# Delta-rule layers: one tile per engine loop, single buffers with copies by ScalarE, and a 64-column set that makes a product and the fourth power

## The chip, the cores and the metric

The kernel runs on one core of one Trainium2 chip. The metric is device time in microseconds (us) of one execution, as the median of several. The engines are PE (TensorE), DVE (VectorE), ACT (ScalarE), POOL (GpSimd) and SP (SyncE); each works through its own list of instructions, and semaphores order them against each other.

## The reference, cut to what matters

The whole model is a chain of a convolution block, a halo attention, a delta-rule transformer, a top-k memory, an attention with mixed heads and a mixture of experts, on 4 x 1024 tokens of 256 channels. The change touches the delta-rule layers alone. There are two of them, with 8 heads of 32:

```python
def delta_rule(q, k, v, beta):
    def step(W, inp):
        qt, kt, vt, bt = inp
        wk = jnp.einsum('bhde,bhe->bhd', W, kt)
        v_new = bt * (vt - wk)
        W = W + jnp.einsum('bhd,bhe->bhde', v_new, kt)
        out = jnp.einsum('bhde,bhe->bhd', W, qt)
        return (W, out)
    W0 = jnp.zeros((bsz, H, D, D), dtype=q.dtype)
    _, outs = jax.lax.scan(step, W0, (q, k, v, beta))
    return outs
...
q = jax.nn.softmax(q, axis=-1); k = jax.nn.softmax(k, axis=-1); beta = jax.nn.sigmoid(beta)
```

## The kernel before, in words

`fast_weight_stage` (L581) runs once per layer. A tile is 32 time steps of all 4 sequences, 128 rows; there are NT = 32 tiles. Within a tile the 32 steps of the scan are solved at once: a lower triangular 32 x 32 system for each of 4 sequences and 8 heads. So nearly all products are *sets* of 32 products of 32 x 32 (8 heads by 4 sequences), which the helper `tiles` (L659) writes out.

Three things run side by side, one tile apart each: the projections and softmax of tile i+1 (`project`, `less_max`, `softmax`), the factors of the triangular system of tile i (`gram`, L673, and five sets called `product`: l8 by l8t, z1 by l2, z2 by l2, tt by l2, z3 by loff), and for tile r = i-1 the recurrence (`chain` sets that read the state M, solve, and step M at L847; then the output `att`). `body(i, ...)` writes one such step for an engine. `bodies` (L613) writes five bodies out, then an engine loop (`Fori`) whose turn holds **four** bodies, then five bodies again; buffers that live longer than a body have four (`qk`, `qkT`, `vh`) or two (`z3`, `nt`, `qm`) places and are indexed by the tile's number mod 4 or 2. The order on each engine is that of the code; PE waits at the head of a set, never inside one.

Other stages have loops too. The mixed-head attention (names with `hm_`) has a PE loop over the four sequences whose body holds an inner loop of six turns (`block_of_queries`): in the built program one inner turn is 748 PE instructions, and the whole body around it 2,486 (each written instruction counted once).

Of the kernel before, what the change touches and what calls it, by code (L numbers as in the profile page):

```python
# [17 lines left out]
P = 128  # L18
# [562 lines left out]
def fast_weight_stage(k, layer, H):  # L581
# [6 lines left out]
    with ExitStack() as ctx:  # L588
# [9 lines left out]
        l8, l8t, loff, z1, z2, tt, l2 = (compact(n) for n in "l8 l8t loff z1 z2 tt l2".split())  # L598
        z3, nt, qm = (sb(n, [P, 2, HEADS, STEP]) for n in ("z3", "nt", "qm"))
        u0, r0, rk, U, M, att = (compact(n) for n in "u0 r0 rk U M att".split())  # L600
        names = ("w power staged pq pv dif exp root qk ga l8 lo qm t l2 z2 tt z3 nt th u0 so r0 rk u m up in att ot fin "
                 "go dch pch").split()
        (s_w, s_power, s_staged, s_pq, s_pv, s_dif, s_exp, s_root, s_qk, s_ga, s_l8, s_lo, s_qm, s_t, s_l2, s_z2, s_tt,
         s_z3, s_nt, s_th, s_u0, s_so, s_r0, s_rk, s_u, s_m, s_up, s_in, s_att, s_ot, s_fin, s_go, s_dch, s_pch) = (
# [8 lines left out]
        def bodies(body, eng, start=None):  # L613

            for i in range(-1, 4):
                body(i, i % 4, i + 1 < NT, i >= 0, i >= 1)
            with eng.Fori(1, NT // 4 - 1) as j:
                if start:
                    start()
                for a in range(4):  # L620
                    body(j * 4 + a, a, True, True, True)
            if start:
                start()
            for i in range(NT - 4, NT + 1):
                body(i, i % 4, i + 1 < NT, i < NT, True)
# [4 lines left out]
        with nc.Block() as block:  # L630
# [5 lines left out]
            def _(pool):  # L636
                own = Steps(pool, s_pch)

                def body(i, a, nxt, ch, rc):
# [15 lines left out]
            def _(pe):  # L655
# [14 lines left out]
                def gram(a):  # L670
                    for n in range(HEADS):
                        for b in range(B):
                            mm = pe.matmul(bank[2][rows(b), 2 * STEP * n:2 * STEP * n + 2 * STEP],  # L673
                                           qkT[rows(b), a, HEADS + n, :], qkT[rows(b), a, n:2 * HEADS:HEADS, :],
                                           start=True, stop=True)
                    mm.then_inc(s_ga, 1)

                of = lambda ap: (lambda n: ap[:, n, :])
                product = lambda left, right: tiles(lambda n: bank[3][:, cols(n)], of(right), of(left), s_t)
                chain = lambda by, moving, sig: tiles(lambda n: bank[4][:, cols(n)], by, of(moving), sig)  # L680

                def body(i, a, nxt, ch, rc):
                    r, ra, ru = i - 1, (a - 1) % 4, (a - 1) % 2
                    if rc:
                        pe.wait_ge(s_m, r + 1)
                        pe.sem_inc(s_go, 1)
                        chain(lambda n: qkT[:, ra, HEADS + n, :], M, s_th)
                    if ch:
# [4 lines left out]
                        gram(a)  # L693
                    if rc:
# [3 lines left out]
                        chain(lambda n: z3[:, ru, n, :], u0, s_so)  # L698
# [3 lines left out]
                    if rc:  # L702
                        pe.wait_ge(s_r0, r + 1)
                        pe.sem_inc(s_go, 1)
                        chain(lambda n: nt[:, ru, n, :], r0, s_so)
# [4 lines left out]
                    if rc:  # L710
                        pe.wait_ge(s_rk, r * 2 + 1)
                        pe.sem_inc(s_go, 1)
                        chain(lambda n: nt[:, ru, n, :], rk, s_so)
                    if nxt:
                        project(i + 1, QKN, 3 * C + HEADS, 1, s_pv)
                    if ch:
                        pe.wait_ge(s_l2, i + 1)
                        pe.sem_inc(s_go, 1)
                        product(z1, l2)
                    if rc:  # L720
                        pe.wait_ge(s_rk, r * 2 + 2)
                        pe.sem_inc(s_go, 1)
                        chain(lambda n: nt[:, ru, n, :], rk, s_so)
                    if ch:
                        pe.wait_ge(s_z2, i + 1)
                        pe.sem_inc(s_go, 1)
                        product(z2, l2)
                    if rc:
                        if since(r, 1):
                            pe.wait_ge(s_att, r)  # L730
                        pe.sem_inc(s_go, 1)
                        tiles(lambda n: bank[6][:, cols(n)], lambda n: qkT[:, ra, n, :], of(M), None, stop=False)
                        pe.wait_ge(s_u, r + 1)
                        pe.sem_inc(s_go, 1)
                        tiles(lambda n: bank[5][:, cols(n)], lambda n: qk[:, ra, C + STEP * n:C + STEP * n + STEP],
                              of(U), s_up)
                    if ch:
                        pe.wait_ge(s_tt, i + 1)
                        pe.sem_inc(s_go, 1)
                        product(tt, l2)  # L740
                    if rc:
                        for n in range(HEADS):
                            for b in range(B):
                                mm = pe.matmul(bank[6][rows(b), cols(n)], qm[rows(b), ru, n, :], U[rows(b), n, :],
                                               start=False, stop=(n == HEADS - 1))
                        mm.then_inc(s_in, 1)
                    if ch:
# [3 lines left out]
                        product(z3[:, a % 2], loff)  # L751
# [13 lines left out]
            def _(act):  # L765
                def body(i, a, nxt, ch, rc):
# [4 lines left out]
                    if ch:  # L771
                        act.wait_ge(s_t, i * 5 + 1)
                        act.activation(flat(l2[:, :, :]), bank[3][:, 0:C], ACT.Copy).then_inc(s_l2, 1)
                    if nxt:
# [10 lines left out]
                    if ch:  # L785
                        act.wait_ge(s_t, i * 5 + 5)
                        act.activation(flat(nt[:, a % 2, :, :]), bank[3][:, 0:C], ACT.Copy, scale=-1.0).then_inc(s_nt, 1)
# [10 lines left out]
            def _(dve):  # L798
# [13 lines left out]
                def softmax(i, a):  # L812
                    dve.wait_ge(s_exp, i + 1)
                    own.done(dve.tensor_reduce(sm[:, :], groups(ex[:, :]), AX.X, ALU.add))
                    own.done(dve.reciprocal(rs[:, :], sm[:, :]))
                    dve.wait_ge(s_root, i + 1)
                    own.mark(dve.tensor_tensor(split(vh[:, a, :]), split(bank[1][:, 0:C]), wide(eb[:, 2, :], HEADS),
                                               ALU.mult))
                    own.done(dve.tensor_tensor(rs[:, HEADS:16], rs[:, HEADS:16], eb[:, 2, :], ALU.mult))
                    own.done(dve.tensor_tensor(groups(qk[:, a, :]), groups(ex[:, :]), wide(rs[:, :], 16), ALU.mult))  # L820
                    dve.transpose(qkT[:, a, :, :].rearrange("p n j -> p (n j)"), qk[:, a, :]).then_inc(s_qk, 1)

                def lower(i):
# [3 lines left out]
                    dve.tensor_tensor(z1[:, :, :], small(2), l8t[:, :, :], ALU.subtract).then_inc(s_l8, 1)  # L827

                def masks(u):
                    dve.tensor_tensor(loff[:, :, :], pairs[:, :, 1, :], off, ALU.mult).then_inc(s_lo, 1)  # L830
                    dve.tensor_tensor(qm[:, u, :, :], pairs[:, :, 0, :], small(3), ALU.mult).then_inc(s_qm, 1)

                def factor(i, n, to, before, sig):
                    dve.wait_ge(s_t, i * 5 + n)
                    dve.tensor_tensor(to, split(bank[3][:, 0:C]), before[:, :, :], ALU.add).then_inc(sig, 1)

                def corrected(r, ra):
                    dve.wait_ge(s_th, r + 1)
                    dve.tensor_tensor(flat(u0[:, :, :]), vh[:, ra, :], bank[4][:, 0:C], ALU.subtract).then_inc(s_u0, 1)  # L839
# [9 lines left out]
                def body(i, a, nxt, ch, rc):  # L849
                    r, ra = i - 1, (a - 1) % 4  # L850
                    if rc:
                        corrected(r, ra)
# [4 lines left out]
                    if ch:  # L857
                        masks(a % 2)
# [4 lines left out]
                    if ch:  # L863
                        factor(i, 2, z2[:, :, :], z1, s_z2)
                    if rc:
                        solution(r, 4, U, s_u)
# [1499 lines left out]
```

## Time and profile before

| what | us |
|---|---|
| median of 3 runs | 5422.78 (5417.58 to 5423.65) |
| profiled execution, its own time | 5467.1 |
| its span, first to last instruction | 5465.3 |
| first delta layer, 328 to 1258 of the span | 930 |
| second delta layer, 1636 to 2552 of the span | 916 |

The profiled execution is 0.8% longer than the median of the runs. In the profile PE is the busiest engine (77% of the span); in the two delta layers all engines have idle time. A line such as `L659 PE MATMUL psum<-fw_M,fw_qkT 32*32 32x32 f32` is a group of matmuls with the tiles that they read; "idle ... <-issue" is time in which the engine waited for nothing that the profile shows.

### The profile page before, as it was taken

How to read it: one execution, taken by the hardware profiler on the slowest of the kernel's cores; microseconds unless marked ns; L12 is line 12 of the kernel's file. 1: busy time of each engine (PE TensorE's matmuls, PEld its weight loads, DVE VectorE, ACT ScalarE, POOL GpSimd, SP SyncE). 2: the span in 40 equal slices, each digit the busy share in tenths (PEclk: the TensorE clock that was granted, in tenths of full speed). 3: DMA queues.
4: the chain of work that ended last, by engine and by line, in shares of the span. 5: the costliest groups of instructions: out<-in, count | busy, mean ns of one | idle time of the engine just before them, and what ended most of it. 6: DMA issues, size and time to landing. Idle time of an engine off the chain costs nothing. (4 is left out here: it accounts for less than half of the span.)

```text
span 5465.3 us, 173116 instructions
## 1 busy us (share of the span) xinstructions
PE 4194.9 (77%) x75148; PEld 2525.7 (46%) x75149; DVE 2689.1 (49%) x5011; ACT 1812.7 (33%) x3259; POOL 877.7 (16%) x2195
## 2 busy tenths in 40 slices
PE   3666666667986666666788887699999999984995
PEld 1235455453435555554245554255454544533663
DVE  3443223233023323332478887378685886852343
ACT  1121111112121111110366665167575775731221
POOL 0000000000000000000155554011111111104012
PEclk7776666667996666666899998799999999995997
DMA  1000000000000000000100000000000000005123
GB/s 41 2 8 4 4 4 4 4 4 18 0 6 4 4 4 4 4 4 5 37 1 1 1 1 1 9 1 0 1 0 1 0 1 1 0 3 210 61 83 101
DMA packets 47696, 88.13 MB, mean 16 GB/s; under 512 B 7120, under 2 KB 38128, under 8 KB 46064
## 3 DMA queue, kind: packets, MB, share of 16 engines
q1 hardware_dynamic: 40944, 61.84, 3.3%
q0 software_dynamic: 6144, 16.79, 0.9%
q8 instruction: 552, 9.04, 0.7%
q14 instruction: 56, 0.46, 0.0%
HBM read 45.05 MB, written 33.55 MB: 14 GB/s over the span
## 5 line engine op out<-in xcount | busy, mean ns | idle before, releaser
L1618 PE MATMUL psum<-hm_ex,hm_mix 128*128 128x512 f32 x1024 | 510.4, 621 | 42.2 <-ACT hm_Aq L1698 38.2
L1684 ACT ACTIVATE hm_ex<-psum,hm_nm 128x1024 f32<-128x1024 f32 x256 | 285.5, 1115 | 297.6 <-DVE hm_nm L1742 297.6
L1752 DVE TENSOR_SCALAR_CACHE_REDUCE hm_plus<-hm_Aq,hm_cbcol,hm_sums 128x1024 f32<-128x1024 f32 x256 | 340.4, 1330 | 0.0
L1618 PEld LDWEIGHTS psum<-hm_ex,hm_mix 128*128 128x128 f32 x1024 | 175.5, 191 | 352.2 <-issue 344.5
L1757 DVE COPY hm_A<-psum 128x1024 f32<-128x1024 f32 x256 | 312.8, 1222 | 51.5 <-PE psum L1627 47.8
L1742 DVE TENSOR_REDUCE hm_nm<-psum 128x1 f32<-128x1024 f32 x256 | 310.9, 1215 | 13.3 <-PE psum L1606 13.3
L1627 PEld LDWEIGHTS psum<-K,hm_Aq 128*128 128x128 f32 x2048 | 236.7, 140 | 149.9 <-issue 145.2
L666 PE MATMUL psum<-fw_w,fw_stage 128*128 128x512 f32 (+1 forms) x512 | 286.8, 697 | 17.7 <-DMA fw_w<-in_slow 16.6
L1689 ACT ACTIVATE hm_junk<-hm_Aq 128x1024 f32<-128x1024 f32 x256 | 270.6, 1057 | 30.3
L1606 PE MATMUL psum<-hm_kt,hm_qd 64*32 64x512 f32 x4096 | 279.8, 605 | 0.0
L1627 PE MATMUL psum<-K,hm_Aq 128*128 128x128 f32 x2048 | 266.6, 273 | 5.6 <-DVE hm_A L1757 5.6
L646 POOL TENSOR_TENSOR fw_eb<-fw_eb,fw_power 128x8 f32<-128x8 f32 x64 | 12.8, 200 | 1595.7 <-ACT fw_ex L778 1595.7
L659 PE MATMUL psum<-fw_M,fw_qkT 32*32 32x32 f32 x8192 | 148.1, 231 | 156.4 <-issue 156.4
L1164 ACT ACTIVATE pt_signs<-pt_acts,pt_tb 128x1024 f32<-128x1024 f32 (+1 forms) x224 | 227.6, 1018 | 113.7 <-POOL pt_tb L1031 93.2
L1698 ACT ACTIVATE hm_Aq<-psum 128x1024 f32<-128x1024 f32 x256 | 259.5, 1014 | 11.2 <-PE psum L1618 11.2
L1078 PE MATMUL psum<-pt_w_proc,pt_keptT 128*128 128x512 f32 x512 | 227.0, 602 | 10.0 <-ACT pt_keptT L1149 10.0
L843 DVE TENSOR_TENSOR fw_rk<-psum,fw_r 128x256 f32<-128x256 f32 x128 | 54.3, 424 | 334.4 <-PE psum L659 334.4
L1535 POOL TENSOR_TENSOR hm_mix<-hm_kron,hm_rinv 128x128 f32<-128x128 f32 x256 | 102.1, 399 | 663.2 <-DVE hm_rinv L1747 663.2
L659 PEld LDWEIGHTS psum<-fw_M,fw_qkT 32*32 32x32 f32 x8192 | 126.2, 144 | 174.5 <-issue 174.5
L2069 ACT ACTIVATE ex_ht<-psum,ex_b 128x128 f32<-128x128 f32 x320 | 91.3, 368 | 324.4 <-PE psum L2001 241.7
L847 DVE TENSOR_TENSOR fw_M<-fw_M,psum 128x256 f32<-128x256 f32 x64 | 27.0, 421 | 339.9 <-PE psum L659 339.9
L839 DVE TENSOR_TENSOR fw_u<-fw_vh,psum 128x256 f32<-128x256 f32 x64 | 27.0, 421 | 337.7 <-PE psum L659 337.7
(360 smaller groups left out, 8207.4 us busy)
## 6 DMA issues: line engine op xcount, KB each, us to landing
ex_rows_in<-ex_zero SPq DMA_DIRECT2D x2, 5120.0 KB, 24.5
ex_xs<-ex_rows_in SPq DMA_DIRECT2D x80, 128.0 KB
ex_rows_out<-ex_ys SPq DMA_DIRECT2D x80, 128.0 KB, 1.7
ex_w<-in_ex_w SPq DMA_DIRECT2D x2, 4096.0 KB
X<-in_x SPq DMA_DIRECT2D x2, 2048.0 KB, 11.0
out_y<-X SPq DMA_DIRECT2D x2, 2048.0 KB, 9.0
ff_w<-in_ff_w SPq DMA_DIRECT2D x2, 1024.0 KB, 5.9
pt_w_proc<-in_pt_proc SPq DMA_DIRECT2D x1, 2048.0 KB, 7.7
```

Of the source, the lines that this page charges most:

```text
L659: mm = pe.matmul(to(n)[rows(b), :], by(n)[rows(b), :], of(n)[rows(b), :], start=start and (stop or n == 0), stop=stop)
L666: mm = pe.matmul(bank[to][:, 0:hi - lo], stage[:, h, :], w[:, h, lo:hi], start=(h == 0), stop=(h == CH - 1))
L1164: act.activation(signs[:, u, 0:n], acts[:, lane(j), u, 0:n], ACT.Sign, bias=tb[:, lane(j), u, 0:1], accum_out=tb[:, lane(j), u, 1:2]).then ...
L1606: mm = pe.matmul(bank[2 * u + c][32 * pr:32 * pr + 32, :], qd[64 * c:64 * c + 64, u, pr, :, :].rearrange("p j n -> p (j n)"), kt[64 * c:64 ...
L1618: mm = pe.matmul(bank[4 + c], mix[:, u, :], ex[:, u, 512 * c:512 * c + 512], start=True, stop=True)
L1627: mm = pe.transpose(bank[6 + m // 4][:, P * (m % 4):P * (m % 4) + P], Aq[:, u, P * m:P * m + P], k.const("ident"))
L1684: act.activation(ex[:, u, :], flat2(psum[:, 2 * u:2 * u + 2, :]), ACT.Exp, bias=nm[:, u:u + 1], accum_out=rsum[:, u:u + 1]).then_inc(s_ex, 1)
L1689: act.activation(junk[:, :], Aq[:, u, :], ACT.Square, accum_out=ssq[:, bass.ds(b * TI + i, 1)]).then_inc(s_sq, 1)
L1698: act.activation(Aq[:, u, :], flat2(psum[:, 4:6, :]), ACT.Copy).then_inc(s_cp, 1)
L1742: dve.tensor_reduce(nm[:, u:u + 1], flat2(psum[:, 2 * u:2 * u + 2, :]), AX.X, ALU.max, negate=True).then_inc(s_nm, 1)
L1752: dve.tensor_scalar(plus[:, :], Aq[:, u, :], cbcol[:, :], sums[:, :], ALU.add, ALU.add, accum_out=sums[:, :]).then_inc(s_run, 1)
L1757: dve.tensor_copy(A[:, :, :, QT_ * t:QT_ * t + QT_], flat2(psum[:, 6:8, :]).rearrange("p (m g n) -> p m g n", m=MT, g=HEADS)).then_inc(s_a ...
```

## The change

1. **The loop.** `bodies` writes three bodies, a `Fori` whose turn is **one** body, and two bodies. PE's loop turn goes from 7,320 instructions to 1,703.
2. **Single buffers.** `qk`, `qkT`, `vh`, `z3`, `nt`, `qm` have one place each. What the recurrence of tile r still needs is copied by ACT into `kc` (keys), `qkTc` (transposed queries and keys) and `vhc` (values). New semaphores `cv`, `ct`, `ck`, `rd` guard the copies; DVE's `qm` waits for `in` of the tile before.
3. **The factors.** Instead of `z1·l2`, then `z2·l2` (copied out as `tt` by ACT), then `tt·l2`, there is one set with 64 moving columns, `fourth()`: l2 against the pair `zl` = (z1, l2 transposed), which gives the product and the transposed fourth power; DVE transposes it to `l4`, and one set `z2·l4` follows. DVE gets two transposes of 128x256; a `product` set and ACT's `tt` go.
4. **Order.** PE's set that reads M for the output (bank 6) moves up to stand behind the first chain set; DVE's `softmax` is split into `sums`, `strengths` and `softmax`, and `mask` moves behind the state.

The diff, cut:

```diff
-        qk = sb("qk", [P, 4, QKN]); qkT = sb("qkT", [P, 4, 2 * HEADS, STEP])
-        vh = sb("vh", [P, 4, C])
+        qk = sb("qk", [P, QKN]); qkT = sb("qkT", [P, 2 * HEADS, STEP]); vh = sb("vh", [P, C])
+        kc = sb("kc", [P, C]); qkTc = sb("qkTc", [P, 2 * HEADS, STEP]); vhc = sb("vhc", [P, C])
...
         def bodies(body, eng, start=None):
-            for i in range(-1, 4):
-                body(i, i % 4, i + 1 < NT, i >= 0, i >= 1)
-            with eng.Fori(1, NT // 4 - 1) as j:
+            for i in range(-1, 2):
+                body(i, i + 1 < NT, i >= 0, i >= 1)
+            with eng.Fori(2, NT - 1) as i:
                 if start:
                     start()
-                for a in range(4):
-                    body(j * 4 + a, a, True, True, True)
+                body(i, True, True, True)
             if start:
                 start()
-            for i in range(NT - 4, NT + 1):
-                body(i, i % 4, i + 1 < NT, i < NT, True)
+            for i in range(NT - 1, NT + 1):
+                body(i, i + 1 < NT, i < NT, True)
...
+                def fourth():
+                    for n in range(HEADS):
+                        for b in range(B):
+                            mm = pe.matmul(halves[rows(b), :, n, :], l2[rows(b), n, :], zl[rows(b), :, n, :],
+                                           start=True, stop=True)
+                    mm.then_inc(s_t, 1)
...
                     if rc:
                         pe.wait_ge(s_m, r + 1)
+                        pe.wait_ge(s_ct, r + 1)
                         pe.sem_inc(s_go, 1)
-                        chain(lambda n: qkT[:, ra, HEADS + n, :], M, s_th)
+                        chain(lambda n: qkTc[:, HEADS + n, :], M, s_th)
+                        tiles(lambda n: bank[6][:, cols(n)], lambda n: qkTc[:, n, :], of(M), s_rd, stop=False)
...
                     if ch:
-                        pe.wait_ge(s_l2, i + 1)
+                        pe.wait_ge(s_l2t, i + 1)
                         pe.sem_inc(s_go, 1)
-                        product(z1, l2)
+                        fourth()
...
-                        product(z2, l2)
+                        product(z2, l4)
                     if rc:
-                        if since(r, 1):
-                            pe.wait_ge(s_att, r)
+                        pe.wait_ge(s_u, r + 1)
+                        pe.wait_ge(s_ck, r + 1)
                         pe.sem_inc(s_go, 1)
-                        tiles(lambda n: bank[6][:, cols(n)], lambda n: qkT[:, ra, n, :], of(M), None, stop=False)
...
-                    if ch:
-                        pe.wait_ge(s_tt, i + 1)
-                        pe.sem_inc(s_go, 1)
-                        product(tt, l2)
...
             @block.scalar
...
+                        act.wait_ge(s_qk, i + 1)
+                        if rc:
+                            act.wait_ge(s_u0, r + 1)
+                        act.activation(vhc[:, :], vh[:, :], ACT.Copy).then_inc(s_cv, 1)
+                        if rc:
+                            act.wait_ge(s_rd, r + 1)
+                        act.activation(flat(qkTc[:, :, :]), flat(qkT[:, :, :]), ACT.Copy).then_inc(s_ct, 1)
...
-                        act.wait_ge(s_t, i * 5 + 3)
-                        act.activation(flat(tt[:, :, :]), bank[3][:, 0:C], ACT.Copy).then_inc(s_tt, 1)
+                        if rc:
+                            act.wait_ge(s_up, r + 1)
+                        act.activation(kc[:, :], qk[:, C:QKN], ACT.Copy).then_inc(s_ck, 1)
...
             @block.vector
...
+                def second(i):
+                    dve.wait_ge(s_l2, i + 1)
+                    dve.transpose(flat(zl[:, 1, :, :]), flat(l2[:, :, :])).then_inc(s_l2t, 1)
+
+                def fourth(i):
+                    dve.wait_ge(s_t, i * 4 + 2)
+                    own.mark(dve.transpose(flat(l4[:, :, :]), bank[3][:, C:2 * C]))
+                    own.sync()
+                    dve.tensor_tensor(z2[:, :, :], split(bank[3][:, 0:C]), zl[:, 0, :, :], ALU.add).then_inc(s_z2, 1)
```

What this makes of PE's list, at the end of one tile in the first layer. Before (fw0 is the first layer; `U` times `qk` and `qm` are the recurrence, the sets with `z` and `tt` the factors), from the second factor set to the transposes of the output; the next tile's first set follows, and the branch comes only after four tiles:

```order
L659 MATMUL psum<-fw0_z1,fw0_l2 32x32 x32
L659 MATMUL psum<-fw0_rk,fw0_nt 32x32 x32
L659 MATMUL psum<-fw0_z2,fw0_l2 32x32 x32
L659 MATMUL psum<-fw0_M,fw0_qkT 32x32 x32
L659 MATMUL psum<-fw0_U,fw0_qk 32x32 x32
L659 MATMUL psum<-fw0_tt,fw0_l2 32x32 x32
L744 MATMUL psum<-fw0_U,fw0_qm 32x32 x32
L659 MATMUL psum<-fw0_z3,fw0_loff 32x32 x32
L757 MATMUL psum<-K,fw0_att 128x128 x2
L659 MATMUL psum<-fw0_M,fw0_qkT 32x32 x32
```

The same place of the changed program; the last two rows are the end of the loop's turn:

```order
L680 MATMUL psum<-fw0_zl,fw0_l2 32x2x32 x32
L730 REGISTER_ALU
L658 MATMUL psum<-fw0_rk,fw0_nt 32x32 x32
L658 MATMUL psum<-fw0_z2,fw0_l4 32x32 x32
L658 MATMUL psum<-fw0_U,fw0_kc 32x32 x32
L744 MATMUL psum<-fw0_U,fw0_qm 32x32 x32
L658 MATMUL psum<-fw0_z3,fw0_loff 32x32 x32
L757 MATMUL psum<-K,fw0_att 128x128 x2
L617 REGISTER_ALU
L617 COMPARE_AND_BRANCH
```

The set of `tt` is gone, the set of `M` by `qkT` has moved to the head of the body, and the branch back stands behind every tile. At the head of the turn the changed program has:

```order
L658 MATMUL psum<-fw0_M,fw0_qkTc 32x32 x64
L698 REGISTER_ALU
L672 MATMUL psum<-fw0_qkT 32x64 x32
L658 MATMUL psum<-fw0_u0,fw0_z3 32x32 x32
L709 REGISTER_ALU
L665 MATMUL psum<-fw0_w,fw0_stage 128x512 x2
```

The 64 in its first row are the chain set and the moved set, back to back on one wait. ACT's list for one tile was (first layer):

```order
L770 ACTIVATE fw0_r0<-psum 128x256
L773 ACTIVATE fw0_l2<-psum 128x256
L777 ACTIVATE fw0_eb<-psum 128x8
L778 ACTIVATE fw0_ex<-fw0_dif 128x512
L781 ACTIVATE fw0_tt<-psum 128x256
L784 ACTIVATE fw0_att<-psum 128x256
L787 ACTIVATE fw0_nt<-psum 128x256
```

and is now:

```order
L773 ACTIVATE fw0_l2<-psum 128x256
L777 ACTIVATE fw0_vhc<-fw0_vh 128x256
L780 ACTIVATE fw0_qkTc<-fw0_qkT 128x512
L782 REGISTER_ALU
L784 ACTIVATE fw0_eb<-psum 128x8
L785 ACTIVATE fw0_ex<-fw0_dif 128x512
L789 ACTIVATE fw0_kc<-fw0_qk 128x256
L792 ACTIVATE fw0_att<-psum 128x256
```

The copies stand between `l2` and `eb` and behind `ex`; `tt` is gone.

## Rows read from the trace of the kernel before

**Rows 1.** Windows, first delta layer: length, busy us (instructions) by engine, clock, DMA, GB/s.

```profile
328.00:1258.00 930.00, 597.16 (x28991) 468.99 (x28992) 280.83 (x641) 96.94 (x257) 70.04 (x98) 0.65 0.02 5
```

**Rows 2.** Waits of PE, first layer: us in total, times, longest us.

```profile
PE psum L659 <- issue: 284.4, 172, 4.0
PE psum L673 <- issue: 15.0, 19, 1.6
...
PE psum L659 <- DVE fw_z L835: 3.7, 7, 1.7
```

**Rows 3.** Timeline of PE around the loop's first branch back: start us, us, instructions.

```profile
541.43 1.06 PE L659 MATMUL psum<-fw_U,fw_qk 32*32 32x32 f32 x64
542.28 0.30 PE L659 MATMUL psum<-fw_tt,fw_l 32*32 32x32 f32 x7
544.48 1.00 PE L659 MATMUL psum<-fw_tt,fw_l 32*32 32x32 f32 x57 [1.90 <-issue]
...
547.88 1.01 PE L659 MATMUL psum<-fw_z,fw_loff 32*32 32x32 f32 x58 [1.24 <-issue]
...
553.28 0.43 PE L659 MATMUL psum<-fw_M,fw_qkT 32*32 32x32 f32 x14 [3.77 <-issue]
556.21 0.90 PE L659 MATMUL psum<-fw_M,fw_qkT 32*32 32x32 f32 x49 [2.50 <-issue]
```

**Rows 4.** Windows between two such gaps, and from one branch to the next.

```profile
544.48:547.88 3.40, 2.16 (x127) 1.94 (x128) 1.66 (x3) 0.38 (x1) 0.00 (x0) 0.50 0.02 5
556.21:663.74 107.53, 72.00 (x3551) 56.45 (x3552) 35.20 (x80) 11.21 (x30) 8.72 (x12) 0.66 0.02 4
```

**Rows 5.** DMA queues, 548 to 664, one turn: packets, MB, share.

```profile
q8 instruction: 31, 0.51, 1.8%
```

**Rows 6.** Timeline of PE around the loop's second branch back.

```profile
663.74 1.01 PE L659 MATMUL psum<-fw_z,fw_loff 32*32 32x32 f32 x58 [1.80 <-issue]
...
671.83 0.90 PE L659 MATMUL psum<-fw_M,fw_qkT 32*32 32x32 f32 x49 [2.22 <-issue]
```

**Rows 7.** Windows, inside the mixed-head stage's inner loop.

```profile
3951.00:4140.00 189.00, 183.60 (x1865) 94.35 (x1863) 165.90 (x230) 142.08 (x219) 37.15 (x88) 1.00 0.00 0
```

**Rows 8.** DMA packets of all queues in that stretch, 3951 to 4140.

```profile
DMA packets 0, 0.00 MB, mean 0 GB/s; under 512 B 0, under 2 KB 0, under 8 KB 0
```

**Rows 9.** DMA queues over one whole sequence of that stage, 3853 to 4180.

```profile
q8 instruction: 12, 0.20, 0.3%
```

**Rows 10.** Timeline of PE, first gap inside a set in the first layer.

```profile
359.08 1.82 PE L673 MATMUL psum<-fw_qkT 32*32 32x64 f32 x60 [1.61 <-issue]
```

**Rows 11.** Timeline of DVE: the state's steps, first and last ones of both layers.

```profile
378.88 0.42 DVE L847 TENSOR_TENSOR fw_M<-fw_M,psum 128x256 f32<-128x256 f32 x1 [6.22 <-PE psum L659]
...
1238.47 0.42 DVE L847 TENSOR_TENSOR fw_M<-fw_M,psum 128x256 f32<-128x256 f32 x1 [5.74 <-PE psum L659]
...
1256.61 0.42 DVE L847 TENSOR_TENSOR fw_M<-fw_M,psum 128x256 f32<-128x256 f32 x1 [3.26 <-PE psum L659]
...
1686.24 0.42 DVE L847 TENSOR_TENSOR fw_M<-fw_M,psum 128x256 f32<-128x256 f32 x1 [6.63 <-PE psum L659]
...
2528.79 0.42 DVE L847 TENSOR_TENSOR fw_M<-fw_M,psum 128x256 f32<-128x256 f32 x1 [4.25 <-PE psum L659]
...
2550.10 0.42 DVE L847 TENSOR_TENSOR fw_M<-fw_M,psum 128x256 f32<-128x256 f32 x1 [3.57 <-PE psum L659]
```

**Rows 12.** Groups of DVE and ACT, first layer: busy us, mean ns | idle before, releaser.

```profile
L821 DVE STREAM_TRANSPOSE fw_qkT<-fw_qk 128x512 f32<-128x512 f32 x32 | 22.8, 711 | 1.1
...
L773 ACT ACTIVATE fw_l<-psum 128x256 f32<-128x256 f32 x32 | 12.3, 383 | 140.9 <-PE psum L659 140.9
```

**Rows 13.** Timeline of PE, sets back to back at the full clock.

```profile
444.39 1.98 PE L666 MATMUL psum<-fw_w,fw_stage 128*128 128x512 f32 x4
446.30 0.75 PE L659 MATMUL psum<-fw_r,fw_nt 32*32 32x32 f32 x64
446.91 0.26 PE L659 MATMUL psum<-fw_l,fw_l8t 32*32 32x32 f32 x7
```

More of the change, by code:

```diff
@@ L668, in project, with gram @@
                     mm.then_inc(sig, 1)
-                def gram(a):
+                def gram():
                     for n in range(HEADS):
@@ L692, in body @@
                         pe.sem_inc(s_go, 1)
-                        gram(a)
+                        gram()
                     if rc:
@@ L697, in body @@
                         pe.sem_inc(s_go, 1)
-                        chain(lambda n: z3[:, ru, n, :], u0, s_so)
+                        chain(of(z3), u0, s_so)
                     if nxt:
@@ L704, in body @@
                         pe.sem_inc(s_go, 1)
-                        chain(lambda n: nt[:, ru, n, :], r0, s_so)
+                        chain(of(nt), r0, s_so)
                     if ch:
@@ L712, in body @@
                         pe.sem_inc(s_go, 1)
-                        chain(lambda n: nt[:, ru, n, :], rk, s_so)
+                        chain(of(nt), rk, s_so)
                     if nxt:
@@ L722, in body @@
                         pe.sem_inc(s_go, 1)
-                        chain(lambda n: nt[:, ru, n, :], rk, s_so)
+                        chain(of(nt), rk, s_so)
                     if ch:
@@ L750, in body @@
                         pe.sem_inc(s_go, 1)
-                        product(z3[:, a % 2], loff)
+                        product(z3, loff)
                     if rc:
@@ L815, in softmax, with strengths @@
                     own.done(dve.reciprocal(rs[:, :], sm[:, :]))
+                def strengths(i):
                     dve.wait_ge(s_root, i + 1)
-                    own.mark(dve.tensor_tensor(split(vh[:, a, :]), split(bank[1][:, 0:C]), wide(eb[:, 2, :], HEADS),
+                    if since(i, 1):
+                        dve.wait_ge(s_cv, i)
+                    own.mark(dve.tensor_tensor(split(vh[:, :]), split(bank[1][:, 0:C]), wide(eb[:, 2, :], HEADS),
                                                ALU.mult))
                     own.done(dve.tensor_tensor(rs[:, HEADS:16], rs[:, HEADS:16], eb[:, 2, :], ALU.mult))
-                    own.done(dve.tensor_tensor(groups(qk[:, a, :]), groups(ex[:, :]), wide(rs[:, :], 16), ALU.mult))
-                    dve.transpose(qkT[:, a, :, :].rearrange("p n j -> p (n j)"), qk[:, a, :]).then_inc(s_qk, 1)
+                def softmax(i):
+                    if since(i, 1):
+                        dve.wait_ge(s_ck, i)
+                    own.done(dve.tensor_tensor(groups(qk[:, :]), groups(ex[:, :]), wide(rs[:, :], 16), ALU.mult))
+                    if since(i, 1):
+                        dve.wait_ge(s_ct, i)
+                    dve.transpose(flat(qkT[:, :, :]), qk[:, :]).then_inc(s_qk, 1)
                 def lower(i):
@@ L857, in body @@
                     if ch:
-                        masks(a % 2)
+                        second(i)
                     if rc:
@@ L863, in body @@
                     if ch:
[L864 removed]
+                        fourth(i)
                     if rc:
                         solution(r, 4, U, s_u)
+                    if ch:
+                        factor(i)
+                    if nxt:
+                        sums(i + 1)
+                    if rc:
                         state(r)
                     if nxt:
[L869 removed]
+                        strengths(i + 1)
                     if ch:
[L871 removed]
+                        mask(i)
+                    if nxt:
+                        softmax(i + 1)
                 dve.memset(M[:, :, :], 0.0).then_inc(s_m, 1)
```

66 lines of the change are left out of this document (32 added, 34 removed).

## The prediction

> **What bounds the kernel now.** I read the windows by stage first. One delta layer takes 930 us, and in it PE shows 597 us of matmuls, DVE 281, ACT 97 and POOL 70 [rows 1]: no engine is full. So the next view is what PE waits for. Of its idle time 284.4 and 15.0 us stand as "issue", in which no data was missing; the largest wait for another engine is 3.7 us [rows 2]. Data bounds next to nothing here.
>
> The timeline shows what the issue gaps are. They fall inside a set: 7 matmuls of the `tt` set, 1.90 us of nothing, then the other 57 [rows 3]. No semaphore is waited for there. Between two such gaps stand 127 matmuls and 128 weight loads [rows 4], with a wait instruction 256 in all. Over one turn of the loop the instruction queue moved 31 packets of 0.51 MB together [rows 5], 16 KB each, which is 256 instructions of 64 bytes. So PE runs 256 instructions, one *line*, and then stands until the next line is fetched. Between 556.21 and 663.74 the 7,103 records shown and the few waits make 28 lines: 107.53 / 28 = **3.84 us a line** [rows 4], whatever the line holds.
>
> At the branch back more is lost: from the start of the turn's last, partial line (547.88) to the start of the target's second line (556.21) pass 8.33 us, at the next branch 8.09 (663.74 to 671.83) [rows 3, 6]. I take 8.2 us a **crossing**. Check: 28 x 3.84 + 8.3 = 115.8, and from 547.88 to 663.74 the trace has 115.9.
>
> Not every loop pays this. In the mixed-head stage's inner loop PE ran 3,728 matmuls and loads in 189 us [rows 7], over five turns, with no packet at all on any queue [rows 8]. Its turn of 748 instructions covers four lines, and entering a line fetches the one behind it, so at least **five** lines stay in the buffer. The loop around it, 2,486 instructions that lie over 11 lines, and the line behind bring 12 packets for every sequence [rows 9]: it is fetched whole each time, so the buffer keeps **fewer than 12**.
>
> **The change part by part.**
>
> *PE's instructions.* A product of 32x32 is two loads and two matmuls, a transpose one of each. The new turn has 420 x 4 + 2 x 2 + 19 others = 1,703 instructions; the old one 7,320 for four tiles, 1,830 each. Where the turn lies in the lines can be worked out: the first gap inside a set, at 359.08 [rows 10], is a line's start, and it comes 944 instructions after the stage's first one, so the stage starts 80 into a line. What is written before the new loop is 2,375 instructions; 80 + 2,375 = 9 x 256 + 151. The turn goes from 151 in its first line to 62 in its eighth. The second layer comes out at 185 to 96, in the same way: eight lines too. With the line behind the last, a turn needs **nine** lines in the buffer.
>
> *Does the buffer keep nine?* The rows bound it: at least 5, at most 11. With 5 to 8 the line behind the loop pushes out the target, the target pushes out the next, and every line is fetched anew in every turn. With 9 to 11 nothing is fetched. Four of the seven possible sizes lose, so I take "not kept", a little above even.
>
> The Trainium skill ("Runtime: NRT & Kernel Launch", section "Instruction fetch mechanics") gives TensorE's instruction memory as 2,048 instructions refilled in blocks of 256. The block agrees with the 256 above; by that size there would be eight lines, and the sum below would hold. The same section says that a taken branch must find its target in a window of two pages; the inner loop of four lines, turned with no packet [rows 8], does not agree.
>
> *The sum when it is not kept.* From the start of a turn's second line to that of the next turn's second line lie six lines and a crossing: 6 x 3.84 + 8.2 = 31.2 us a tile. The state is stepped 32 times a layer. Of the 31 intervals, 28 hold a branch: 28 x 31.2 = 875. The first and the last but one are straight code: 1,703 / 256 x 3.84 = 25.5 each. The last has the recurrence alone, and I keep what it takes now, 18.1 and 21.3 us [rows 11]. That makes 944 us from first to last step in the first layer, where the trace has 1256.61 - 378.88 = 877.7, and 947 in the second, where it has 863.9 [rows 11]: +66 and +83. Ahead of the first step two sets fewer, one line, save 3.8 us a layer. Together **+142 us**.
>
> *Work added on DVE and ACT: nothing.* DVE gets two transposes of 128x256 a tile. The trace has none; half of the 128x512 one is 0.36 us, the whole 0.71 [rows 12], so 0.7 to 1.4 us a tile, and I take 0.8. ACT gives up one copy of 0.38 [rows 12] and gets three; of 128x256 that is 0.38 as now, of 128x512 at most twice that: about 1.2 us more. DVE is idle for 20 of a tile's 29 us and ACT for 26 [rows 1], and PE's fetching is the cover. Where the copies are waited for: the chain set at the turn's head waits for `qkTc`, made a tile earlier; `U` by `kc` waits for a copy made 25 us before. Behind the state, DVE's `qk` waits for `kc`, and `gram` for `qkT`; that is 0.4 + 0.7 + 0.7 after the `up` set, under two sets, the transposes, the crossing and two more sets, over 10 us. If the fetching went, this cover would shrink to those sets, about 3 us, and still hold.
>
> *The 64-column set.* It has 32 products as well, so in instructions it costs what a 32-column set costs. The factor chain loses one set and one copy and gains two transposes; it runs beside fetching that takes 3.84 us a line, so nothing of it shows.
>
> **The rivals.**
>
> 1. *The buffer keeps the loop* (the other sign). Then no packet comes in a turn and PE's own work bounds the tile. A set takes 446.91 - 446.30 = 0.61 us at the full clock [rows 13] and 542.28 - 541.43 = 0.85 at the half [rows 3]; the wide projection 1.91 at the full [rows 13], estimated double at the half. Eleven sets, two 64-column sets at up to twice a set, both projections (the second half as wide) and the transposes make about 12 us at the full clock and 19 at the half. The recurrence needs six sets and six evictions in a row, 8 to 10 us, and fits under it. With waits between links I take 16.5 (13 to 19.5). For: five kept lines are seen, and nothing seen speaks against nine. Against: nothing seen speaks for nine. The layers then take 28 x 16.5 + 51 + 18 = 531 and 534, so -347 - 330 - 8 = -684: **4739 us** (4543 to 4907). It decides at nine lines. The skill's 2,048 instructions named above, read as a limit on a loop's length, would give this case, since 1,703 is less.
> 2. *Only a part is fetched anew.* If a miss replaced some other line than the next one needed, a turn would pay a crossing and little more, about 22 us: 5047 us. Against: all 12 packets came in the loop of 11 lines [rows 9].
> 3. *No change.* The turn would have to come out at 28 to 29 us, by lines of about 3.4, as one single line shows [rows 4]; the mean over 28 lines speaks against it.
>
> **How the numbers follow.** The profiled execution is 0.8% longer than the median of the runs; I add the difference to the median: 5422.8 + 142 = **5565 us**. Its own range: a line at 3.6 gives 86 us less, an uncovered microsecond in each turn 56 more, so 5480 to 5630. Chances: the forecast 0.55, rival 1 0.36, rival 2 0.07, no change (within 0.2%, about what a measurement of this kernel can tell) 0.02. So slower 0.55, the same 0.02, faster 0.43. As both signs hold much, the range reaches into rival 1, leaving out its lowest part and the top of the forecast: **4650 to 5620**.
>
> **What would show it.** Right: in the new loop the state's steps stand 31 us apart, PE's issue gaps stay and one of 3 to 4 us stands at every tile's first set, and a layer moves about 280 packets (9 a turn, 20 for the straight code) on the instruction queue. Wrong: if a layer moves some 30 packets and the steps are 13 to 20 us apart, the buffer kept nine lines, and the step that failed is the choice between 5 and 11. If packets come but steps are below 28 us, the price of a line or of a crossing was wrong. If the gaps of PE are put down to ACT's copies or DVE's transposes, the cover was.

## The result, and the profile after

The changed kernel takes **5344.49 us** (median of 4 runs, 5341.95 to 5354.78), the kernel before in the same comparison 5421.28 us. The ratio is 0.9863, 95% interval 0.9845 to 0.988: **1.4% faster, 77 us**. The forecast was 5565 us and slower. The profiled execution took 5342.08 us, its span is 5340.3.

The two layers went opposite ways. The windows run from the first to the last step of the state in the first and in the second layer, then over two turns of the first layer (columns as in [rows 1]; the third row is a turn from branch to branch, the fourth runs from there to the start of the next turn's last line):

```profile
375.82:1100.16 724.34, 497.77 (x25801) 399.23 (x25803) 286.39 (x662) 116.51 (x302) 62.93 (x86) 0.73 0.01 3
1526.34:2471.01 944.67, 548.52 (x25817) 425.76 (x25820) 289.21 (x662) 116.48 (x302) 62.91 (x86) 0.65 0.02 5
404.62:419.38 14.76, 14.20 (x864) 11.87 (x855) 7.29 (x18) 3.86 (x10) 2.18 (x3) 0.85 0.00 0
419.38:451.70 32.32, 18.71 (x813) 14.24 (x814) 11.77 (x28) 3.85 (x10) 2.18 (x3) 0.65 0.02 5
```

Against the 877.7 and 863.9 us that [rows 11] give, that is -153 and +81, together -72.6, close to the 77 us between the medians. (The two spans differ by 125 us; 46 of these lie behind the last step of the second layer, in code that the change doesn't touch, and the profiled execution of before was 0.8% longer than its median.) The timeline of DVE, the state's steps (those of [rows 11] are at L847, these at L878):

```profile
375.82 0.42 DVE L878 TENSOR_TENSOR fw_M<-fw_M,psum 128x256 f32<-128x256 f32 x1
...
401.11 0.42 DVE L878 TENSOR_TENSOR fw_M<-fw_M,psum 128x256 f32<-128x256 f32 x1 [2.02 <-PE psum L658]
...
418.99 0.42 DVE L878 TENSOR_TENSOR fw_M<-fw_M,psum 128x256 f32<-128x256 f32 x1
...
448.94 0.42 DVE L878 TENSOR_TENSOR fw_M<-fw_M,psum 128x256 f32<-128x256 f32 x1 [0.76 <-PE psum L658]
...
1709.82 0.42 DVE L878 TENSOR_TENSOR fw_M<-fw_M,psum 128x256 f32<-128x256 f32 x1 [0.34 <-PE psum L658]
...
1741.21 0.42 DVE L878 TENSOR_TENSOR fw_M<-fw_M,psum 128x256 f32<-128x256 f32 x1 [0.67 <-PE psum L658]
...
1772.13 0.42 DVE L878 TENSOR_TENSOR fw_M<-fw_M,psum 128x256 f32<-128x256 f32 x1 [1.73 <-PE psum L658]
```

In the second layer the steps stand 31.4 and 30.9 us apart, and so all 28 loop turns of it (30.2 to 32.5). In the first they **alternate**: 17.9, 30.0, and so on, 14 turns of 16.8 to 18.4 us and 14 of 28.0 to 30.0.

The DMA queues say why. The instruction queue over the first layer's steps, over the second's, and all packets of the first layer between two branches, 404.6 to 419.5:

```profile
q8 instruction: 143, 2.34, 1.4%
...
q8 instruction: 270, 4.42, 2.1%
...
DMA packets 0, 0.00 MB, mean 0 GB/s; under 512 B 0, under 2 KB 0, under 8 KB 0
```

Before, both layers moved about 230 packets (31 for four tiles, [rows 5]). Now the second layer moves nine lines a turn, the first half as many: a turn in which nothing is fetched (I call it *held*) stands between two that fetch nine lines. The timeline of PE shows both ends of a held turn:

```profile
404.27 0.64 PE L658 MATMUL psum<-fw_z,fw_loff 32*32 32x32 f32 x30 [1.99 <-issue]
404.85 0.69 PE L757 MATMUL psum<-K,fw_att 128*128 128x128 f32 x2
405.46 1.93 PE L658 MATMUL psum<-fw_M,fw_qkTc 32*32 32x32 f32 x128
...
419.29 0.44 PE L757 MATMUL psum<-K,fw_att 128*128 128x128 f32 x2
424.16 0.87 PE L658 MATMUL psum<-fw_M,fw_qkTc 32*32 32x32 f32 x49 [4.43 <-issue]
427.50 1.28 PE L658 MATMUL psum<-fw_M,fw_qkTc 32*32 32x32 f32 x79 [2.48 <-issue]
```

At 404.27 PE enters the loop's last line after a gap of 1.99 us, branches back behind the transposes and has the next turn's first set at once: no crossing, no gap. That turn ends at 419.29; there the crossing is paid (4.43 and 2.48 us), and the gaps of a fetched turn follow. The trace's records of the two branches, which the views leave out, differ in the same way: 0.21 us at 404.62, 4.51 us at 419.38. PE's waits of the first layer, to compare with [rows 2]:

```profile
PE psum L658 <- issue: 191.3, 89, 5.0
PE psum L672 <- issue: 19.0, 16, 1.7
PE psum L658 <- DVE fw_z L861: 14.2, 27, 1.1
```

The issue gaps of these two groups went from 299 to 210 us; one small wait is new, 0.5 us a tile for `z2`, which now stands behind a transpose.

**Theory A**, from this reading: the buffer keeps exactly eight lines. A loop of eight is refetched whole if the line behind it is asked for, and held if not. In the first layer the last line has 62 instructions (the *tail*) and it isn't asked for in every other turn; in the second it has 96 and always is. **Theory B**: the alternation comes from data or waits, or from fewer than eight lines.

### The profile page after: what moved, and what is told of

The parts are those of the page before. It is cut to its first block and busy times, and to the rows that moved or that the text cites. A ratio compares the mean times of both kernels' runs of the same rounds, so it can differ in the third digit from the quotient of the medians.

```text
span 5340.3 us, 166254 instructions
## 1 busy us (share of the span) xinstructions
PE 4097.5 (77%) x71052; PEld 2447.9 (46%) x71053; DVE 2742.2 (51%) x5139; ACT 1867.5 (35%) x3387; POOL 874.9 (16%) x2195
## 5 line engine op out<-in xcount | busy, mean ns | idle before, releaser
L658 PE MATMUL psum<-fw_M,fw_qkTc 32*32 32x32 f32 x8192 | 134.4, 236 | 283.4 <-issue 283.4
L658 PEld LDWEIGHTS psum<-fw_M,fw_qkTc 32*32 32x32 f32 x8192 | 121.2, 149 | 309.2 <-issue 309.2
L770 ACT ACTIVATE fw_r<-psum 128x256 f32<-128x256 f32 x64 | 24.6, 384 | 615.3 <-PE psum L658 615.3
L870 DVE TENSOR_TENSOR fw_u<-fw_vhc,psum 128x256 f32<-128x256 f32 x64 | 26.9, 421 | 400.5 <-PE psum L658 400.5
```

Source lines behind the costliest of these rows:

```text
L658: mm = pe.matmul(to(n)[rows(b), :], by(n)[rows(b), :], of(n)[rows(b), :], start=start and (stop or n == 0), stop=stop)
```

## The experiments

Tails are worked out as in the prediction; a padding of n instructions moves the loop by n - 1. The traces bear the counts out: from the gap at the start of the last line up to and with the branch they have four instructions more than the tail worked out (66 for 62 here, 103 for 99 in run 2, 10 for 6 in run 13). Dead work adds to the kernel and leaves nothing out.

**1. Seven lines.** Increments of a semaphore that nobody waits for, ahead of PE's first body:

```diff
                 pe.wait_ge(s_w, 16)
+                for _ in range((130, 0)[layer]):
+                    pe.sem_inc(s_go, 1)
                 bodies(body, pe)
+                for _ in range((0, 126)[layer]):
+                    pe.sem_inc(s_go, 1)
```

> 130 increments of a semaphore that nobody waits for are written ahead of PE's bodies in the first layer (126 more behind the second layer's loop put later stages back on their places in the lines). They shift both loops: the turn of 1,703 instructions then lies over 7 lines in both layers, from 24 and 58 in its first line, where the changed kernel has 8. Theory A (the buffer keeps exactly eight lines, and what is refetched depends on whether the line behind the loop is asked for): 7 lines and the one behind fit, no packet in the loops, steps of the state 16.5 to 17.5 us apart as in the changed kernel's held turns; a layer then takes 28 x 17 + 51 + 18 = 545 us, against 724 and 945 now, so -579: about 4765 us (4740 to 4800). Theory B (fewer than eight lines are kept, and the first layer's alternation comes from elsewhere): every turn is refetched over 7 lines, 5 x 3.84 + 8.2 = 27.4 us, both layers 836 us: about 5345 us.

Measured: **4622.85 us**, ratio 0.8521 (0.8503 to 0.8539). Both layers are held from the second loop turn on, 13.76 us a tile; 451 and 450 us. Theory B's small buffer is out, and the 17 us that I took from held turns was too much: those followed a fetched turn.

**2. A longer tail**: the same with 38 and 218.

> 38 such increments: the turns keep 8 lines in both layers, but the instructions in the last line go from 62 to 99 in the first layer (the second had 96 and gets 133). Theory A (the line behind the loop is asked for only if PE stays in the last line long enough, and only then is the whole loop refetched): the alternation of 17.5 and 29 us in the first layer goes, all turns of both layers take 31.2 us; the first layer goes from 724 to 944 us and the second stays at 945: 5342 + 220 = about 5562 us, what was forecast for the change itself. Theory B (the alternation has another cause, a wait or the data of every second tile): nothing moves, 5342 us.

Measured: 5630.47 us, ratio 1.038 (1.0357 to 1.0402). The alternation is gone: all 28 turns of the first layer take 29.4 to 33.9 us, and its packets are those of the second:

```profile
q8 instruction: 270, 4.42, 2.1%
```

The first layer takes 965 us, its turns 32.0 on average; the second 940. Theory A holds: the same instructions, 38 places further on, cost the first layer 240 us. What lies above 5562 is mostly the paddings: 130 increments had put the first step from 375.82 to 395.35, 0.15 us each, so by estimate 256 are 38 us; the first layer's longer turns add 21.

**3. Short tails in both layers**: the shift now by dead products, which cost PE less:

```diff
+                for j in range((222, 0)[layer] // 4):
+                    c = j % B
+                    pe.matmul(bank[7][rows(c), 0:STEP], w[rows(c), 0, 0:STEP], w[rows(c), 0, 0:STEP], start=True, stop=True)
+                for _ in range((222, 0)[layer] % 4):
+                    pe.sem_inc(s_go, 1)
```

> 55 dead 32x32 products and two semaphore increments (222 instructions) ahead of PE's bodies in the first layer: 8 lines in both layers as in the changed kernel, but with 27 and 61 instructions in the last line instead of 62 and 96. Theory A (short last line: the line behind isn't asked for in a turn that is late, and the next turn is held): the second layer now alternates too and goes from 945 to about 720 us, the first stays near 724: 5344 - 225 + 1 = about 5120 us. Theory B (the two layers differ for another reason than the place of the loop in its lines): the second layer stays at 945 us, 5345 us.

Measured: 5105.98 us, ratio 0.9402 (0.9386 to 0.9419). The second layer (tail 61) alternates too, 721 us; the first (tail 27) takes 697. It no longer alternates strictly: 12 of its 28 turns are fetched, and three times two or three held turns stand together. So what set the layers apart is where their loops lie.

**4. The 64-column set alone**, in the loop of four tiles:

```diff
-                        product(z1, l2)
+                        fourth()
...
-                        product(z2, l2)
+                        product(z2, l4)
...
-                        product(tt, l2)
```

> The kernel before with its loop of four tiles and its buffers, and of the change the 64-column set alone (with DVE's two transposes; one product set and ACT's copy tt go). Theory A (PE is bound by its lines, 3.84 us per 256 instructions): 129 instructions a tile fewer are 1.94 us, 62 us a layer, 124 in all: 5421 - 124 = about 5297 us. Theory B (the two transposes lie on the path of the factors and are waited for): 0.8 to 2 us a tile are given back, 5350 to 5425 us.

Measured: 5364.84 us against 5424.96, ratio 0.9893 (0.9871 to 0.9916): -60, half of theory A and within theory B's range. PE's waits of its first layer show a new one:

```profile
PE psum L660 <- issue: 180.5, 113, 4.3
PE psum L660 <- DVE fw_z L847: 68.6, 30, 3.3
```

L847 writes `z3`, which DVE makes behind the next tile's softmax; the wait is for `z3` and not, as theory B had it, for the transposes. So the forecast's "nothing of it shows" does not hold for this set by itself; run 10 asks what the wait costs.

**5. The old factors in the one-tile loop** (the three `product` lines of run 4 back, `l4` and the transposes out).

> The changed kernel with its one-tile loop, single buffers and copies, but with the factors of before (three product sets and the copy tt, no transposes). The turn has 1,832 PE instructions, lies over 8 lines in both layers and has 193 and 231 instructions in its last line. Theory A: the line behind is always asked for, all turns are refetched at 6 x 3.84 + 8.2 = 31.2 us whatever the lines hold; both layers 28 x 31.2 + 2 x 27.5 + 18 = 947 us and a line more ahead of the loop: 5342 + 223 + 2 + 8 = about 5575 us. Theory B (a turn costs by its instructions: 129 more are 1.94 us, and the first layer alternates as now): 5342 + 2 x 62 = about 5465 us.

Measured: 5684.45 us, ratio 1.0481 (1.0458 to 1.0504). Every turn is refetched, at 32.9 us (993 and 987 us a layer). Theory A, with a turn 1.7 us dearer than it said (93 us in all). So loop, single buffers and order without the set cost 260 us, more than the 142 that the forecast charged to the whole change. They were not run apart from each other.

**6. A late `att`**, first layer, ACT:

```diff
                         act.wait_ge(s_in, r + 1)
+                        if layer == 0:
+                            for j in range(9):
+                                act.activation(spare[:, j, :], bank[6][:, 0:C], ACT.Copy)
```

> The changed kernel, its loops where they are; in the first layer alone ACT makes nine dead copies of bank 6 (9 x 0.38 = 3.4 us) ahead of att, so that PE, in the late turns too, stands in the last line and waits for att until about 1 us after it entered it. Its last line keeps 62 instructions. Theory A, by time (what decides whether the line behind is asked for is how long PE stays in the last line): no turn of the first layer is held any more, about 32 us each, 28 x 32.3 + 69 = 973 us instead of 724: 5344 + 249 = about 5590 us. Theory A', by count (62 instructions are too few, however long they take): the alternation stays, with the held turn longer by up to 3.4 us: about 5390 us.

Measured: 5377.89 us, ratio 0.9904 (0.9886 to 0.9922), alternation as before (742 us). It decides nothing: the copies run back to back at 0.28 us, and the transposes behind PE's last line waited for nothing. Run 9 mends it.

**7. No loop**:

```diff
-            with eng.Fori(2, NT - 1) as i:
+            for i in range(2, NT - 1):
```

> The changed kernel without a loop: all 33 bodies written out on every engine. It prices a line without a crossing. By the terms of the forecast (1,703 / 256 x 3.84 = 25.5 us a tile, nothing for branches) a layer takes 30 x 25.5 + 18 = 783 us from first to last step, against 724 and 945: 5344 + 59 - 162 = about 5241 us. If instead part of the 8.2 us of a crossing is the price of the lines themselves, a line comes to about 4.2 us and a tile to 28: 858 us a layer, about 5391 us.

Measured: 5277.86 us, ratio 0.9717 (0.97 to 0.9735). 25.9 and 25.8 us a tile (30 steps, without the last) against 25.5: the price of a line without a branch was right within 2%, and written-out code beats the changed kernel by 67 us.

**8. Seven lines, cheaply**: run 1 with run 3's padding, 131 instructions.

> The run with 7 lines again, with the shift made by 32 dead 32x32 products and three increments (131 instructions) instead of 130 increments, and no second padding behind the second layer. Theory A: a single increment costs PE about 0.15 us (130 of them put the first step of the state from 375.8 to 395.4), a dead product next to nothing; the loops are held as there at 13.76 us a tile: 4623 - 39 = about 4585 us. Theory B: the shift of the first step came from the other place of the straight code in the lines, and the paddings cost nothing: about 4620 us.

Measured: **4575.41 us**, ratio 0.8428 (0.8412 to 0.8444), as theory A had it (4585), the fastest version here, 769 us under the changed kernel. Windows, DMA packets and PE's waits over ten turns:

```profile
500.00:637.60 137.60, 124.63 (x8437) 102.38 (x8430) 93.36 (x221) 38.55 (x101) 21.84 (x30) 1.00 0.00 0
...
DMA packets 0, 0.00 MB, mean 0 GB/s; under 512 B 0, under 2 KB 0, under 8 KB 0
...
PE psum L672 <- DVE fw_qkT L844: 6.5, 10, 0.7
PE psum L658 <- DVE fw_z L866: 5.4, 10, 0.5
```

No packet, PE busy 12.46 of 13.76 us at a granted clock of 1.00 (2.4 GHz throughout; the second layer of the changed kernel has 0.65). What it waits for is DVE: 0.65 us a turn for `qkT`, 0.54 for `z2`. `z2` stands right behind an added transpose, so there the work added on DVE shows; that `qkT` comes later because of it is not shown.

**9. A later `att`**: run 6 with 16 copies.

> The run with the late att again, with 16 dead copies of bank 6 ahead of att in the first layer instead of nine: eight of those took 2.32 us, about 0.28 each, and att was there when PE reached its last line (408.10, the transposes ran at 408.68 without a wait), so that run delayed nothing and decided nothing. 16 make about 4.6 us, and PE should stand in its last line of 62 instructions until about 410.5, 2.4 us after entering it. Theory A, by time: the line behind is asked for, no turn of the first layer is held, about 33 us each: 28 x 33 + 69 = 993 us instead of 724, about 5610 us. Theory A', by count: the alternation stays, held and late turns each 2 to 4 us longer, 5344 + 28 x 3 = about 5430 us.

Measured: 5447.62 us, ratio 1.0041 (1.0024 to 1.0057). PE and ACT at the end of a fetched turn, and the packets from 406.9 to 424.8:

```profile
407.03 0.65 PE L658 MATMUL psum<-fw_z,fw_loff 32*32 32x32 f32 x30 [1.75 <-issue]
409.68 0.69 PE L757 MATMUL psum<-K,fw_att 128*128 128x128 f32 x2 [2.00 <-ACT fw_att L795]
...
404.81 4.53 ACT L794 ACTIVATE fw_spare<-psum 128x256 f32<-128x256 f32 x16 [0.20 <-PE psum L744]
...
DMA packets 0, 0.00 MB, mean 0 GB/s; under 512 B 0, under 2 KB 0, under 8 KB 0
```

PE stood in its last line for 2.65 us before the transposes, against under a microsecond without the copies; the line behind was not asked for, and the next turn was held. The branch was not taken early either: the trace has it at 409.77, 2.74 us after PE entered the line. Turns of about 20 and 32.5 us alternate. **Theory A by time falls**; with runs 2 and 3 that leaves the tail's count of instructions (A').

**10. Run 4 with `z3` early**:

```diff
                         solution(r, 4, U, s_u)
+                    if ch:
+                        factor(i, a)
+                    if rc:
                         state(r)
...
-                    if ch:
-                        factor(i, a)
```

> The four-tile loop with the 64-column set alone, and DVE's last factor (z3) moved from the end of the body, behind the next tile's softmax, to ahead of the state's step, as the change has it. Without this move PE waited 59 us of the first layer for z3. Theory A (that wait ate the missing half of what two lines fewer a turn should give): the wait goes, 5421 - 124 = about 5297 us (5285 to 5320). Theory B (the lines themselves became dearer, or the branch): as without the move, 5365 us.

Measured: 5321.90 us against 5423.45, ratio 0.982 (0.9803 to 0.9836): -102, just above the range of theory A. The wait for `z3` is gone (L843 writes `z2`), and the line gaps are back:

```profile
PE psum L660 <- issue: 225.4, 139, 4.3
...
PE psum L660 <- DVE fw_z L843: 12.9, 25, 0.5
```

The set with its order brings most of what two lines fewer a turn are worth (124 us), and beats the whole change without touching loop or buffers.

**11. Tails of 72 and 82**: paddings of 11 and 233 as in run 3.

> The changed kernel with 11 instructions of padding in the first layer and 233 in the second (dead 32x32 products and one to three increments): 8 lines in both layers, with 72 and 82 instructions in the last line. 27, 61 and 62 alternated; 96, 99 and 133 were refetched in every turn. Theory A puts the border at some time in the last line between 0.35 and 0.69 us, so between 62 and 96: if 72 still alternates and 82 does not, about 5345 us; if both alternate, 5125; if neither does, 5565. Theory B (no border; what layer alternates has another cause): the first layer alternates and the second not, whatever the tails, 5345 us with the first layer's turns unchanged.

Measured: 5132.25 us, ratio 0.9465 (0.9449 to 0.9481): both alternate strictly, 723 and 727 us. The instruction queue from 375 to 1100, in the first layer:

```profile
q8 instruction: 144, 2.36, 1.5%
```

The border lies between 82 and 96 instructions.

**12. The copies twice**: in run 8, a dead copy ahead of each of ACT's three.

```diff
+                        act.activation(spv[:, :], vh[:, :], ACT.Copy)
                         act.activation(vhc[:, :], vh[:, :], ACT.Copy).then_inc(s_cv, 1)
```

> The cheap 7-line version with each of ACT's three new copies made twice (a dead one ahead of the real one, into buffers of its own). It asks whether the copies cost anything once the cover of the fetching is gone. Theory A (hidden beside PE, which is busy 12.5 of a tile's 13.76 us): 13.76 us a tile as without them, about 4575 us. Theory B (the copies stand in the path through the state and softmax to the next gram set): 0.38 to 1.4 us a tile more, 56 tiles, 4596 to 4653 us.

Measured: 4581.49 us, ratio 0.8449 (0.8435 to 0.8463); 13.77 us a tile. ACT's copies are hidden even when nothing is fetched.

**13. Tails of 6 and 12**: paddings of 201 and 229 as in run 3.

> 8 lines in both layers with 6 and 12 instructions in the last line (201 and 229 instructions of padding, dead 32x32 products and one increment each). In the run with a late att PE stood 2.6 us in a last line of 62 instructions and the line behind still wasn't asked for, so the time there doesn't decide. Theory C (PE's reader runs some tens of instructions ahead of what PE executes, 83 to 96 by the tails so far, and the line behind is asked for only if the reader stays in the last line; in a held turn it stays because PE hasn't taken what it read): with a tail much shorter than that it leaves the line at once in held turns too, and nothing is refetched: 13.76 us a tile in both layers although the loop has 8 lines, about 4580 to 4700 us. Theory D (only late turns skip the request, whatever the tail; held turns always ask): both layers alternate as with 27 and 61, about 5110 us.

Measured: 4888.13 us, ratio 0.9002 (0.8987 to 0.9017); the profiled execution took 1.3% more, so that its counts need not be those of the others. Between C and D: there 8 and 10 of 28 loop turns are refetched, where tails of 61 to 82 have 14. From 405.0 to 463.3, over four turns of an eight-line loop:

```profile
DMA packets 0, 0.00 MB, mean 0 GB/s; under 512 B 0, under 2 KB 0, under 8 KB 0
```

So eight lines do stay, and held turns don't always ask for the ninth. D is out; C's direction holds, its "nothing is refetched" doesn't.

## Why the prediction was wrong

- **What bounds the layers**: right. Lines at 3.84 us gave 25.5 us a written-out tile; run 7 has 25.8 and 25.9. 129 instructions a tile fewer brought 102 of 124 us (run 10). One reading was off without harm: the largest wait for another engine was not 3.7 us but one of 5.7, for the first tile's `qkT`.
- **The buffer keeps fewer than nine**: right, and the number is eight: seven lines and the one behind are held (run 8), eight and the one behind are not (run 2), eight alone are (run 13). The prediction chose this by counting four of seven possible sizes, so that it came out right is partly luck. The Trainium skill ("Runtime: NRT & Kernel Launch", section "Instruction fetch mechanics") states 2,048 instructions for TensorE; these runs agree with that size. It also says that crossing a block is mostly hidden and that branches favour full unrolling; the traces do not agree: against the first stand 236 us of issue gaps in the first layer's 796 us of written-out code (run 7), against the second a loop that beats this code by 702 us (runs 7 and 8).
- **The failed step** is in the prediction's "Does the buffer keep nine?": "the line behind the loop pushes out the target ... and every line is fetched anew in every turn", taken from "entering a line fetches the one behind it" and applied to both layers alike. The second layer came out at 944.7 us where 947 was forecast. The first took 724 instead of 944, since with a tail of 62 every other turn doesn't ask for that line. These 220 us are the miss: 5565 - 220 = 5345. The tails, 62 and 96, stood in the prediction, but were used only to count lines. The result lies inside the stated range by luck: the range joined two outcomes, all turns fetched or none, and half the turns of one layer were held, which neither foresaw. The sign given for a wrong price, packets with steps below 28 us, came up as well, though the prices were right.
- **The crossing and the turn**: 31.2 us forecast; where every turn was refetched a layer's turns took 31.3 us on average here and 31.1 to 33.0 in runs 2 and 5, and the second layer moved 270 packets where some 280 were forecast.
- **Added work at nothing**: right for ACT (run 12). For DVE nearly right where every turn is fetched (PE waited 3.2 us for `z2` in 720 us of run 2); here it waits 0.5 us a tile in the first layer, and once nothing is fetched 1.2 of 13.76 us for DVE (run 8).
- **Rival 1**: 16.5 us a tile for a held loop; 13.76 measured. PE's work was priced rightly (12 us, 12.46 measured), the waits not (4.5, 1.3 measured).

What the parts bring is not a sum: one-tile loop with old factors +260 us, the set with `z3` early but without the loop -102, both -77, both with seven lines -855 (against the before of each comparison). By the count of lines, the set's worth in the one-tile loop is that 1,703 instructions can lie on seven lines and 1,832 cannot; no run has the old factors on a short tail.

**Left open**: what it is about the count of instructions in the last line. Theory C of run 13 fits most readings: a reader in PE that runs some tens of instructions ahead and asks for the next line only if it doesn't meet the branch first. The traces show the branch only a little ahead of the matmuls (at 404.62, 0.22 us before the first transpose), no run shows a reader that far ahead, and tails of 6 and 12 still let some held turns ask.

## What to carry to other kernels

Where a profile puts PE's gaps down to issue, count the instructions between the gaps and the packets of the instruction queue before anything else. Then place the hot loop: work out in how many 256-instruction lines it lies, leave room for the line behind, and shift it by a few cheap instructions; here seven lines instead of eight were worth 14% of the kernel. A change of loop length also moves all later code in its lines, so measure it at more than one place before crediting the change itself.

## What the runs showed of the hardware

- PE's instructions come in lines of 256, 3.84 us each here; a loop on seven lines turned without a packet (run 8), one on eight was refetched whole whenever the line behind it was asked for.
- How often a loop of eight lines was refetched fell with its tail: in 28 of 28 turns with 96 and more instructions, in 12 to 14 with 27 to 82, in 10 and 8 with 12 and 6. The tail does not settle it alone: executions of run 13 took 4886 to 4952 us.
- How long PE stood in the last line of a fetched turn made no difference: 2.65 us with 62 instructions brought no packet (run 9).
- A semaphore increment written alone cost PE 0.15 us; 32 dead products and three increments (131 instructions) moved the first step by 0.6 us.
- Over ten held turns in a row the granted clock is 1.00 and PE's own work 12.46 us a turn (run 8); a held turn between fetched ones has 0.85 and 14.20 of 14.76 us, a fetched stretch 0.65 and 18.71 of 32.32 us. Without the gaps PE is also faster at its own work.
